# Mixture-of-experts layers on one core: a wait for the preceding pair's scatters between the two scatters of a pair

## What is computed

```python
x = x + _L0_xattn_ref(_layernorm(x), ctx_2048, ...)
x = x + _L0_ffn_ref(_layernorm(x), ...)   # 16 experts, 2 per token, inner size 64, and a shared expert
x = x + _L1_xattn_ref(_layernorm(x), ctx_2048, mask_BxS2_ik0, ...)
x = x + _L1_ffn_ref(_layernorm(x), ...)   # 32 experts, 4 per token, inner size 128, clipped gate and up
```

## Time and profile before

| what | us |
|---|---|
| median of three runs | 1790.75 (1789.1 to 1797.8) |
| the profiled execution | 1794.14 |
| its span, first to last instruction | 1792.3 |
| its mean granted TensorE clock, as a share of 2.4 GHz | 0.942 |
| experts 0, first scatter to the end | 134.8 |
| experts 1, first scatter to the start of the last | 260.7 |
| all 240 scatters' time on POOL | 244.2 |

### The profile page before, as it was taken

How to read it: one execution, slowest core, us unless ns; L and a number is a source line. 1 busy time by engine, 2 the same in 40 slices (tenths; PEclk the granted TensorE clock), 3 DMA queues, 4 the chain that set the end, 5 groups by cost and what they waited for, 6 DMA issues and landing times.

```text
span 1792.3 us, 44037 instructions
## 1 busy us (share of the span) xinstructions
PE 1540.6 (86%) x14968; PEld 1240.6 (69%) x14968; DVE 1333.8 (74%) x2901; ACT 1095.3 (61%) x3516; POOL 1093.1 (61%) x1111
## 2 busy tenths in 40 slices
PE   4999999999999999989967765898895179998976
PEld 4888888888888888866646652565563169998955
DVE  4889998998998998977533434688877248887876
ACT  3888888888888888843334533665551056666610
POOL 2676676666766766746635554537776636665642
PEclk9999999999999999989989985999996579999988
DMA  6500000000000000022245425102212955554456
GB/s 182 172 20 19 19 20 19 13 18 20 19 20 20 20 20 20 8 95 75 88 156 159 143 76 182 48 32 93 82 70 102 322 162 162 160 160 136 140 196 274
DMA packets 103082, 167.67 MB, mean 94 GB/s; under 512 B 20223, under 2 KB 75980, under 8 KB 102480
## 3 DMA queue, kind: packets, MB, share of 16 engines
q1 hardware_dynamic: 77136, 105.37, 19.3%
q0 software_dynamic: 22272, 56.15, 8.5%
q10 hardware_dynamic: 3456, 3.34, 0.5%
HBM read 95.31 MB, written 75.76 MB: 95 GB/s over the span
## 4 chain that ended last, share of the span: by engine, by line
PE 60%; issue 12%; POOL 10%; DVE 7%; DMA 4%; another core or an unknown queue 2%; ACT 2%; ACTq 1%; SPq 0%; POOLq 0%; DVEq 0%
PE layers_banks L323 13%; PE layers_banks L297 13%; PE layers_banks L309 9%; PE layers_banks L879 7%; POOL l_rows_in L1168 5%; PE layers_banks L890 4%; PE layers_banks L282 3%; PE layers_banks L286 3%; DMA l_rows_in<-layers_arena,l_routing_group_slots 3%; POOL l_by_token L999 2%; PE layers_banks L867 2%; PE layers_banks L2136 1%; PE layers_banks L1618 1%; PE layers_banks L1258 1%
## 5 line engine op out<-in xcount | busy, mean ns | idle before, releaser
L461 POOL TENSOR_TENSOR w_down<-w_down,layers_arena 128x1024 f32<-128x1024 f32 x256 | 484.0, 1895 | 233.6 <-DVE layers_arena L420 232.8
L387 ACT ACTIVATE w_down<-layers_banks,layers_arena 128x256 f32<-128x256 f32 x1024 | 469.5, 498 | 1.8 <-DVE layers_arena L414 1.8
L999 POOL DMA_INDIRECT l_by_token<-layers_arena x240 | 244.2, 1018 | 195.1 <-issue 104.5
L425 DVE COPY w_down<-layers_banks 128x1024 f32<-128x1024 f32 x256 | 312.0, 1219 | 39.7 <-PE layers_banks L309 36.1
L414 DVE TENSOR_REDUCE layers_arena<-layers_banks 128x4 f32<-128x1024 f32 x256 | 309.4, 1209 | 40.8 <-PE layers_banks L297 40.3
L297 PE MATMUL layers_banks<-layers_arena 64*128 64x256 f32 x2048 | 278.8, 385 | 3.0 <-ACT w_down L387 1.8
L323 PE MATMUL layers_banks<-w_down,layers_arena 128*64 128x256 f32 x2048 | 250.4, 386 | 1.8 <-DVE w_down L425 1.3
L387 ACT ACTIVATION_READ_ACCUMULATOR w_down<-layers_banks,layers_arena 128x1 f32 x1024 | 237.9, 232 | 0.0
L879 PE MATMUL layers_banks<-layers_arena 128*128 128x128 f32 x1600 | 206.4, 282 | 30.7 <-ACT layers_arena L922 24.8
L1168 POOL DMA_INDIRECT l_rows_in<-layers_arena,l_routing_group_slots x192 | 191.3, 996 | 57.7 <-issue 45.3
L309 PEld LDWEIGHTS layers_banks<-ident,w_down 64*128 64x128 f32 x4096 | 168.1, 138 | 77.5 <-issue 71.2
(11 more groups left out here) (227 smaller groups left out, 2556.5 us busy)
## 6 DMA issues: line engine op xcount, KB each, us to landing
layers_arena<-l_rows_in SPq DMA_DIRECT2D x240, 136.0 KB
weights<-l_by_token SPq DMA_DIRECT2D x32, 512.0 KB, 9.2
layers_arena<-in_ctx SPq DMA_DIRECT2D x64, 128.0 KB, 2.8
layers_arena<-l_by_token SPq DMA_DIRECT2D x32, 256.0 KB, 2.7
weights<-in_w_gu SPq DMA_DIRECT2D x16, 512.0 KB
l_rows_in<-zeros SPq DMA_DIRECT2D x1, 4352.0 KB
x_sb<-in_x SPq DMA_DIRECT2D x32, 128.0 KB
w_down<-in_w_down SPq DMA_DIRECT2D x1, 4096.0 KB
```

What stands on the lines that cost most here:

```text
L387: last = nc.scalar.activation(prob[:, n % 4, c, :], ps_s[:, n % 2, c, :], ACT.Exp, bias=negmax[:, n % 2, c:c + 1], accum_out=sums[:, n % 2 ...
L425: nc.vector.tensor_copy(prob_t[:, n // 2 % 2, n % 2, :, :, :].rearrange("p k c (d s) -> p d (k c) s", d=2), ps_t[:, :, :, :].rearrange("p ...
L461: nc.gpsimd.tensor_tensor(prob[:, n % 4, :, :], prob[:, n % 4, :, :], rsum[:, n % 2, :].unsqueeze(2).to_broadcast([P, 4, A_N]), ALU.mult). ...
L999: pool.indirect_dma_start(m.by_token, bass.IndirectOffsetOnAxis(ap=place, axis=0), outs[:, r % OUTS, b, :], None, bounds_check=T * m.K - 1 ...
```

## The change

Between the first and the second scatter of each pair but the first, POOL waits until `rows_stored` of the preceding pair shows both of its scatters landed. It holds for both layers.

```diff
--- before.py
+++ after.py
@@ -995,6 +995,8 @@
             done(pool, y_ready, it, r)
             pool.sem_inc(passed, 1)
             for b in range(2):
+                if b == 1 and r > 0:
+                    pool.wait_ge(rows_stored[(r - 1) % OUTS], 32 * ((r - 1) // OUTS + 1))
                 place = dest[:, r % TAILS, b:b + 1].bitcast(I32)
                 pool.indirect_dma_start(m.by_token, bass.IndirectOffsetOnAxis(ap=place, axis=0),
                                         outs[:, r % OUTS, b, :], None, bounds_check=T * m.K - 1, oob_is_err=False)\
```

## The result

The changed kernel takes 1815.4 us in the median (1810.1 to 1824.8, four runs), the kernel before in the same comparison 1792.1; the ratio is 1.0139 (95% interval 1.0090 to 1.0188), some 25 us slower. The prediction was 1792.8 with a range from 1776 to 1809; the result lies above it.

A forecast was written before the change was run, and what follows sets the result against it. The prediction saw layer 0's experts waiting for hand-overs and PE pacing layer 1; terms 0 (layer 0 and ends) + 0 + 2 (layer 1's lateness) on 1790.75 gave 1792.8 us, range 1776 to 1809.

The forecast's parts named there:

- What bounds the kernel: Whole span: 60% chained on PE, 10% on POOL; a POOL change reaches the time only where a scatter ends last.
- Price of one wait: POOL, both layers: the next scatter starts 0.18 us after the awaited landing, read from the routing; 0.86 kept for the range.
- the far end: Upper value for restart, 0.86 us, from VectorE's hand-over to layer 0's first scatter, with two waiting instructions before it.
- Layer 0 and both ends: Quiet queues: 2.12 + 0.18 = 2.30 against 2.58 between second scatters, so the wait costs 0; bound +2.4 us.
- the bound of 2.98: Quiet-queue distance between second scatters if restart takes 0.86 us: 0.40 late per pair.
- The 1.2 us per end: Bound at each stage end, where the last four pairs run back to back: 3 x 0.40 us on the chain.
- Layer 1, steady: Wait met after 3.0 to 3.6 us against 3.25 to 3.28 between second scatters: no slack, on average 0.1 late.
- Eight pairs are 26 us, so a shift reaches nobody: VectorE's `weigh` waits for scatters eight pairs later, so a shift of a microsecond reaches nobody through those semaphores.
- What lateness costs: Layer 1: scatters hold back PE's signals, so a second scatter d later lengthens a pair by d/2; +2 us (0 to +4).
- the faster rival: The gap between scatters lets PE's signals through in both layers: -12 us, 1778.8 us, chance 0.25.
- The slower rival: The wait paces layer 1 through landings lengthened by row loads: 3.41 us per pair, +15 with ends, 1805.8 us, chance 0.28.
- Its tail, 1828: Slower rival's case that landings don't shrink in layer 1: 79 x 0.47 = +37 us, left out of the range.

## Why the prediction was wrong

*What bounds the kernel.* Right that a scatter counts only where it ends last; but that was taken from the kernel before. With the wait, POOL ends both stages 22 us behind the last `weigh`.

*Price of one wait.* **This term failed.** It was taken as 0.18, with 0.86 as the far end; it is 0.76. The row with the same releaser was misread. POOL's timeline before shows what stands ahead of that scatter:

```profile
821.41 0.18 POOL L1164 COPY layers_arena<-weights 128x4 f32<-128x4 f32 x1
821.88 1.13 POOL L1168 DMA_INDIRECT l_rows_in<-layers_arena,l_routing_group_slots  x1 [0.29 <-DMA l_rows_in<-layers_arena,l_routing_group_slots]
```

A copy ends at 821.59 and the scatter follows 0.29 behind it. The same 0.29 stands where the copy itself is the releaser, so the scatter of 821.88 was most likely ready to go, and the landing at 821.70 only happened to lie between:

```profile
836.47 1.14 POOL L1168 DMA_INDIRECT l_rows_in<-layers_arena,l_routing_group_slots  x1 [0.29 <-POOL layers_arena L1164]
```

No scatter in the trace of before is seen to start on a landing alone. The end that was called further off, by two waiting instructions, was the near one.

*Layer 0 and both ends.* The landing of 2.12 was right (2.11). With 0.76 the quiet distance is 2.87, near the bound of 2.98, and not below 2.58. The 1.2 us per end left out what follows: not four pairs but seven stand behind the last `weigh`, and they cost 15 to 16 us more at each end.

*Layer 1, steady.* Landings of 2.8 to 3.4 occur (2.83, 3.00 and 3.39 in the chain above) and were exceeded by 3.71, but they are not the common ones: half of the second scatters come 3.22 or less after the one before, which with 0.76 leaves 2.46 at most for the landing. A landing that was too long and a restart that was too short offset one another: 3.0 to 3.6 was said for the next scatter, and the middle one comes at 3.22. That is luck. What it hid is that the wait binds nearly always and the long landings come on top, which makes 3.52 on average.

*Eight pairs are 26 us, so a shift reaches nobody.* **The second error, and the one that the time goes through**: 15.9 of layer 1's 18.8 lie in the queue. The sentence holds for one shift. POOL's 0.97 of room per pair was the room without the wait; with it 3.25 - 3.20 leaves 0.05, shifts add up, and after half of layer 1 they reach `weigh`. The steady distance with the wait should have been held against the pace first, and the queue at the end priced by the eight buffers.

*What lateness costs.* The loop by which a later scatter lengthens a pair by d/2, the only term that wasn't 0, wasn't seen. PE went the other way: before it was stopped by the full queue it ran at 3.09 per pair for stretches,

```profile
1481.02 1.95 PE L879 MATMUL layers_banks<-layers_arena 128*128 128x128 f32 x16
...
1484.11 1.95 PE L879 MATMUL layers_banks<-layers_arena 128*128 128x128 f32 x16
```

and at 3.17 on average over 39 pairs from 1471.75 on, against 3.21 before, and VectorE's waits for PE in `clip` fell from 34.3 + 8.5 to 22.7 + 2.1. That fits the faster rival's mechanism, and in layer 0 the computing became 13.5 us faster; it was outweighed since the scatters, not PE, end the stage.

*The slower rival* named the right mechanism and place, 1805.8, but not the queue that most of the time goes through. Its T of 3.41 is 3.52 on average in the trace, from other parts: the restart was short by 0.58, and its landing of 3.54 is longer than most. That the two sums are near each other is luck in part. Its tail, 1828, was left out of the range, and the result lies between the two. Its chance of 0.28 rested on the 0.18.

The Trainium skill, "DMA: Bandwidth & Descriptors", section "Rules for kernel authors" (issue early, wait late), pointed the right way. The Trainium skill, "DMA: Bandwidth & Descriptors", section "Anatomy of one DMA — SWDGE (gpsimd) path", has a fixed part of about 2.0 us, by which the wait would be met early. The landings of 2.44 to 3.71 in the chain don't agree with that while the stage runs. The Trainium skill, "SBUF — State Buffer", section "SBUF: two separate sides", says of its ports that PE and ACT wait on nobody. The 16.05 us behind 19 scatters stand against reading this as a promise that PE's hand-overs are on time. Which part of the chip holds them, no run here shows.

## What to carry to other kernels

Price a wait on one's own transfer as landing plus restart, both from a row in which the same kind of instruction truly starts on the landing, and set the sum against the stage's pace: what is above it isn't hidden by buffers, it is stored in them and paid at the end, by as many pairs as there are buffers. A wait that thins out a busy queue can help the other engines at the same time, so look at where each engine finishes, not only at the total; here a fixed piece of work between transfers gave that gain without the queue. The same room paid in layer 0, where PE is busy for 95.01 of 134.81 us, and cost some 20 us in layer 1, where PE is busy for 248.66 of 262.78: try it stage by stage.

## What the runs showed of the hardware

- From the landing of a scatter to the start of the next that waits for it: 0.76 us, 0.50 of it between two instructions of POOL's sequencer.
- A scatter of 128 rows of 1 KB lands in 2.11 us in a quiet queue and in 2.44 while the stage runs; among row loads of 136 KB a landing of 3.71 is on the chain, and one of 4.00 with the loads cut to 8 KB.
- While scatters run without a gap, hand-overs from PE come late: 16.05 us of idleness behind 19 scatters, and 16 matmuls of PE take 9.0 us instead of 1.95. Scatters 1.48 us apart, or 2.98 per pair, let layer 0 run in 126.6 and 126.7 instead of 132.7; 1.37 apart did not.
- Over the first 160 us of layer 1 the granted clock is 1.00 (2.4 GHz) before and after. The lower mean after, 0.95 (0.99 before), comes mainly from the end: behind the last `weigh` PE is busy for 1.01 us of 22.05, and the granted clock there is 0.50 (1.2 GHz):

```profile
1727.56:1749.61 22.05, 1.01 (x4) 0.43 (x4) 5.54 (x7) 0.59 (x1) 14.95 (x15) 0.50 0.02 1
```
